# TensorE's column-half blocks in one run per pass, with the banks and the copy order that go with it

## The reference

```python
qkv = x @ W_attn + b_attn                       # x: 2 x 2048 x 256, 16 heads of 16
scores = einsum('bhtd,bhsd->bhts', q, k) / 4    # causal, and s >= t - 64
out = softmax(scores) @ v ; x = layernorm(x + out @ W_proj + b_proj)
expert_idx = argmax(softmax(x @ Wr.T))          # 8 experts
inter = gelu(x @ W1[expert_idx] + b1[expert_idx])
y = layernorm(inter @ Wo + bo + x) * gamma + beta ; result = layernorm(x + y)
```

## Time and profile before

| | us |
|---|---|
| median of 3 executions | 529.68 (529.24 to 534.57) |
| profiled execution | 528.38 |
| its span, first to last instruction | 526.7 |
| TensorE busy | 489.4 (93%) |
| VectorE busy | 431.5 (82%) |
| ScalarE busy | 356.5 (68%) |
| POOL busy | 315.4 (60%) |
| mean granted TensorE clock | 0.979 |

### The profile page before, as it was taken

The page is one execution under the profiler, slowest core; times in us unless marked ns, Lnnn a source line. Parts: engine busy times, 40 slices in busy tenths (PEclk is TensorE's granted clock), DMA queues, the critical chain, the costliest instruction groups (busy, mean ns, idle before and its releaser), DMA issues. The chain is left out here.

```text
span 526.7 us, 24512 instructions
## 1 busy us (share of the span) xinstructions
PE 489.4 (93%) x8574; PEld 432.2 (82%) x8574; DVE 431.5 (82%) x1132; ACT 356.5 (68%) x796; POOL 315.4 (60%) x553
## 2 busy tenths in 40 slices
PE   6989999999999999899978898999999999999980
PEld 5878888788888888688866787888999989999970
DVE  6558798878987898669898567999999989999983
ACT  5677778777876878467867664566667757666860
POOL 8612446444464545434634347777888878888883
PEclk9999999999999999989999898999999999999996
DMA  8687688786977797768772122222235554442200
GB/s 200 165 245 198 185 220 205 204 217 180 259 211 213 196 255 197 188 191 222 174 205 72 44 61 62 71 64 63 77 105 183 206 182 162 163 147 71 53 25 7
DMA packets 90184, 80.96 MB, mean 154 GB/s; under 512 B 36502, under 2 KB 83871, under 8 KB 90018
## 3 DMA queue, kind: packets, MB, share of 16 engines
q1 hardware_dynamic: 86720, 70.95, 48.9%
q0 software_dynamic: 3248, 8.41, 4.7%
q10 hardware_dynamic: 98, 0.04, 0.0%
HBM read 43.50 MB, written 23.55 MB: 127 GB/s over the span
## 5 line engine op out<-in xcount | busy, mean ns | idle before, releaser
L1415 PE MATMUL ps<-v_even,w_hi 128*128 128x128 f16 x1024 | 142.1, 220 | 0.6 <-issue 0.3
L1397 PE MATMUL ps<-wo_hi,ks 128*128 128x256 f16 (+1 forms) x576 | 129.2, 274 | 6.4 <-DVE ks L1091 6.1
L834 ACT ACTIVATE probs<-ps,b1T 128x128 f32<-128x128 f32 (+1 forms) x312 | 85.8, 361 | 66.9 <-PE ps L1415 66.7
L1415 PE MATMUL ps<-v_even,w_lo 128*128 128x128 f16 x512 | 108.6, 220 | 0.1
L1415 PEld LDWEIGHTS ps<-v_even,w_hi 128*128 x1024 | 97.2, 98 | 3.4 <-issue 1.3
L1162 DVE TENSOR_REDUCE mx<-ps 128x4 bf16<-128x512 f32 x128 | 82.5, 682 | 3.7 <-PE ps L1466 2.5
L1397 PE MATMUL ps<-wo_lo,ks 128*128 128x256 f16 (+1 forms) x288 | 78.9, 274 | 0.0
L1091 DVE TENSOR_TENSOR ks<-probs,ks 128x512 f16<-128x512 f32 (+1 forms) x72 | 70.9, 985 | 5.9 <-ACT ks L841 5.6
L853 ACT ACTIVATE probs<-ps 128x512 f32<-128x512 f32 x128 | 69.5, 610 | 5.3 <-PE ps L1492 4.4
L1515 PE MATMUL ps<-v_odd,probs 128*64 128x17 f32 x1024 | 69.4, 210 | 2.0 <-issue 2.0
L744 POOL CAST att_hi<-att 128x256 f16<-128x256 f32 x27 | 10.7, 395 | 100.9 <-DVE att L1219 100.9
(11 more groups left out here) (248 smaller groups left out, 1283.3 us busy)
## 6 DMA issues: line engine op xcount, KB each, us to landing
qk_s<-qk_room SPq DMA_DIRECT2D x32, 256.0 KB, 2.7
w_in<-in_L_ffn_W_dram SPq DMA_DIRECT2D x16, 512.0 KB, 5.7
v_odd<-slots SPq DMA_DIRECT2D x64, 128.0 KB
qs<-qk_s SPq DMA_DIRECT2D x16, 384.0 KB
ks<-qk_s SPq DMA_DIRECT2D x16, 384.0 KB, 5.5
ks<-qk_s SPq DMA_DIRECT2D x32, 144.0 KB, 3.2
v_even<-v_odd SPq DMA_DIRECT2D x63, 68.0 KB, 3.1
qk_s<-qk_room SPq DMA_DIRECT2D x32, 128.0 KB, 2.7
```

The costliest lines, as they stand in the source:

```text
L834: last = nc.scalar.activation(g[1 - p][:, ic, n * w:(n + 1) * w], ps_h[1 - p][:, half, col + n * w:col + (n + 1) * w], ACT.Gelu, bias=b1T[ ...
L1397: ins = mm(ps_y[p][0:m], h[p][hs][:, ic, 0:m], wo[ws][:, ic, :], start=n == 0, stop=n == 3 * IC - 1)
L1415: up_ins = mm(ps_h[1 - p][:, half, col + m * w:col + (m + 1) * w], weights(ws, m, k, ic), sT[1 - p][ss][:, k, at], start=k + n == 0, stop= ...
```

## The change

On TensorE the projection and the turn of x now stand in front of scores 0 and 1, so that scores 0 and 1, values 0, scores 2 and 3 and values 1 follow each other (only pass 0 keeps the scores first). The maxima's tile is 128 wide instead of 32, so its transposes are too, and ScalarE reads the first 32 partitions of the result. The projection writes bank 6 (the values' bank) except for the last tile, the ranks bank 2 except for the last pair, x's turn bank 4. On VectorE y and logits stand before maxima 0, `router_x` behind attT and waits for the product instead of the copy; the low halves of w1 come as two in even passes (one right behind mean and variance, one behind `router_x`) and none in odd ones. On ScalarE the last exponential of a tile and the copy of v stand in the next pass, behind x's high part, and exponential 0 stands behind the high part of queries and keys.

```diff
-        mx = [sb(f"mx{k}", [P, P - ALIGNED], bf16) for k in range(2)]
+        mx = [sb(f"mx{k}", [P, P], bf16) for k in range(2)]
...
-            return ps[:, 0 if t >= LEAD else 4 + t % 2, 0:CC * P].rearrange("p (k t) -> p k t", k=CC)
+            return ps[:, 4 if t >= LEAD else 4 + t % 2, 0:CC * P].rearrange("p (k t) -> p k t", k=CC)
...
-        ps_proj = ps[:, 1, 0:C + E]
+        def ps_proj(t):
+            return ps[:, 6 if t < TILES - 1 else 1, 0:C + E]
...
-        ps_rank = ps[:, 1, 320:320 + 3 * E].rearrange("p (a e) -> p a e", a=3)
+        def ps_rank(pair):
+            return ps[:, 2 if pair < TILES // 2 - 1 else 1, 320:320 + 3 * E].rearrange("p (a e) -> p a e", a=3)
...
+        def w1_lows(it):
+            lows_at = range(it - 2, it if it % 2 == 0 else it - 2) if it < TILES - 3 else w1_halves(it)
+            return [n for n in lows_at if a_tile(n)]
... ScalarE
                 for t in turned(it) if it > FIRST else ():
                     x_high(t)
+                if a_tile(it - 1) and it < LAST - 2:
+                    exps(3, it - 1)
+                if a_tile(it) and it > 0:
+                    copy_v(it)
...
-                if a_tile(it + 1):
-                    m = it + 1
-                    act.wait_ge(v_done, m + 1)
...
-                if cur:
-                    exps(0)
...
                 if cur:
+                    exps(0)
                     exps(1)
-                if cur:
                     exps(2)
-                    exps(3)
... VectorE
-                    dve.wait_ge(v_out, m + 1)
+                    dve.wait_ge(v_done, m + 1)
...
+                for n in w1_lows(it)[:1]:
+                    split_w1(n)
...
-                for n in w1_halves(it):
+                if it >= 0 and a_tile(it + 1):
+                    router_x(it + 1)
+                for n in w1_lows(it)[1:]:
                     split_w1(n)
... TensorE
-                        wait(pe, att_done, done)
+                        wait(pe, lg_done, done)
...
-                    wait(pe, lg_done, old + 1)
                     wait(pe, v_out, m)
-                    wait(pe, lx_done, m)
...
                 if it == 0:
                     warm(10)
-                scores(0)
+                    scores(0)
+                    scores(1)
                 if a_tile(old):
                     pe.wait_ge(attT_out, old + 1)
...
-                scores(1)
                 for t in turned(it):
                     pe.wait_ge(xin_ld[t % 3], 16 * (t // 3 + 1))
                     if t >= LEAD:
-                        pe.wait_ge(qkh_done, t)
-                        pe.wait_ge(qkl_done, t)
+                        wait(pe, exp_done, 4 * (it - 1) + 1)
...
+                if it != 0:
+                    scores(0)
+                    scores(1)
                 values(0)
                 scores(2)
                 scores(3)
...
-                    pe.wait_ge(v_out, upto(it + 1))
-                    pe.wait_ge(lx_done, upto(it + 1))
+                    if a_tile(it):
+                        pe.wait_ge(mxT_out, 2 * it + 2)
```

More of the change, by code:

```diff
@@ L859, in maxima_rows, with copy_v @@
                     nc.scalar.activation(q.rearrange("p (i h) n -> p i h n", i=STRIPS),
-                                         ps_mx.rearrange("p e m n -> p (e m) n").unsqueeze(1)
+                                         ps_mx[0:P - ALIGNED].rearrange("p e m n -> p (e m) n").unsqueeze(1)
                                          .broadcast_to([P - ALIGNED, STRIPS, 2 * CC, BLK]),
                                          ACT.Copy, scale=1.0 / ONE).then_inc(mxT_out, 1)
+                def copy_v(m):
+                    act.wait_ge(v_done, m + 1)
+                    act.wait_ge(lx_done, m + 1)
+                    if m == 0:
+                        act.wait_ge(v_clear, 1)
+                    wait(act, pv_done, CC * (m - VRING + 1))
+                    wait(act, vtop_ld[m % 2], 16 * ((m - VRING) // 2 + 1))
+                    wait(act, vlow_ld[(m + 1) % 2], 16 * ((m - VRING) // 2 + 1))
+                    nc.scalar.activation(
+                        v_odd[m % VRING][:, :, 0:HD], ps_v[:, 0:C].rearrange("p (h d) -> p h d", d=HD), ACT.Copy)\
+                        .then_inc(v_out, 1)
                 new, sent = it + LEAD, it - 3
                 if it == LAST - 2:
+                    exps(3, it - 1)
                     nc.scalar.activation(table_in[:, :], zero[0:1, :], ACT.Gelu)
@@ L946, in _ @@
                         copy_rows(1, e, t)
+                    copy_v(0)
             walk_slots(body3)
@@ L1180, in router_x @@
                 def router_x(m):
-                    dve.wait_ge(v_out, m + 1)
+                    dve.wait_ge(v_done, m + 1)
                     wait(dve, lg_done, m - 3)
                     nc.vector.tensor_tensor(lx[:, m % 4, :], ps_v[:, C:C + E], lb[:, :], ALU.add).then_inc(lx_done, 1)
+                if a_tile(old):
+                    dve.wait_ge(proj_done, old + 1)
+                    dve.wait_ge(xrb_done, old + 1)
+                    wait(dve, x1_done, old - 1)
+                    nc.vector.scalar_tensor_tensor(y[old % 2][:, :], ps_proj(old)[:, 0:C], W_DOWN, xin[old % XRING],
+                                                   ALU.mult, ALU.add).then_inc(y_done, 1)
+                    dve.wait_ge(lx_done, old + 1)
+                    wait(dve, is_top_done, old // 2)
+                    nc.vector.tensor_tensor(logits[:, old % 2, :], ps_proj(old)[:, C:C + E], lx[:, old % 4, :], ALU.add)\
+                        .then_inc(lg_done, 1)
                 maxima(0)
@@ L1189, in _ @@
                     x_low(t)
[L1190 to L1199, removed]
                 if it == FIRST:
@@ L1440, in scores @@
                     if step == 0:
+                        wait(pe, place_done, (done - 1) // 2)
                         pe.wait_ge(stack_ld[pair % 2], 16 * (pair // 2 + 1 + window_loads(pair)))
@@ L1538, in _ @@
                     warm(10)
-                scores(0)
+                    scores(0)
+                    scores(1)
                 if a_tile(old):
                     pe.wait_ge(attT_out, old + 1)
-                    wait(pe, v_out, upto(it))
-                    wait(pe, lx_done, upto(it))
-                    wait(pe, place_done, old // 2)
+                    if old == TILES - 1:
+                        pe.wait_ge(v_out, TILES)
+                        pe.wait_ge(place_done, old // 2)
                     if old == 0:
                         pe.wait_ge(wlo_done, 4)
-                    product(ps_proj, [(attT[:, 0, c, :], attT[:, 1, c, :]) for c in range(CC)],
+                    product(ps_proj(old), [(attT[:, 0, c, :], attT[:, 1, c, :]) for c in range(CC)],
                             [(wp[0][:, c, :], wp[1][:, c, :]) for c in range(CC)]).then_inc(proj_done, 1)
-                scores(1)
                 for t in turned(it):
@@ L1659, in _ @@
                     pe.wait_ge(onehot_done, old // 2 + 1)
[L1660 to L1663 removed]
+                    if a_tile(it):
+                        pe.wait_ge(mxT_out, 2 * it + 2)
+                    if old == TILES - 1:
+                        pe.wait_ge(lg_done, TILES)
+                    rank = ps_rank(old // 2)
+                    both = rank[:, 0:2, :].rearrange("p a e -> p (a e)")
                     mm(both, before[:, :], onehot[:, 1:3, :].rearrange("p a e -> p (a e)"), start=True, stop=False)
                     mm(both, ones_b[:, :], onehot[:, 0:2, :].rearrange("p a e -> p (a e)"), start=False, stop=True)
[L1666 to L1667 removed]
+                    mm(rank[:, 2, :], ones_b[:, :], onehot[:, 1, :], start=True, stop=False)
+                    mm(rank[:, 2, :], ones_b[:, :], onehot[:, 2, :], start=False, stop=True).then_inc(rank_done, 1)
                 scores_t(2)
```

22 lines of the change are left out of this document (5 added, 17 removed).

## The result

| | before | changed |
|---|---|---|
| median, us | 530.44 (529.24 to 534.57, 4 runs) | 549.15 (546.76 to 555.41, 4 runs) |
| ratio, 95% interval | | 1.0324 [1.0243, 1.0405] |
| profiled execution, span | 528.38, 526.7 | 546.76, 545.0 |
| granted TensorE clock, mean | 0.979 | 0.958 |

The changed kernel is 3% slower; the forecast was 522.5, within 514 to 532. The ratio compares executions in the same state and leaves out the changed kernel's longest, 555.41.

A forecast was written before the change was run, and what follows sets the result against it. TensorE's issue order was taken to set the 8.15 us pass. Saving 0.46 us a pair over 13 pairs (6.0) plus 1.2 in the tail, 7.2, gave 521.2 profiled, 522.5 as median; range 514 to 532.

The forecast's parts named there:

- TensorE's own saving: Attention loop: six column-width changes fewer per pass take 0.65 us off TensorE's work, 8.15 to 7.50 us.
- the sum: All terms added: a pair of passes from 16.30 to 15.84 us over 13 pairs, plus 1.2 in the tail, 7.2 together.
- About 26 passes (tiles 2 to 27) in that state: Attention loop: these passes were taken to last 8.15 us each, with TensorE busy throughout.
- Maxima's wider load, nothing: Maxima's transposes: the weight load four times wider runs under the matmuls and costs nothing.
- Logits before values 0, 0.07 us a pass: Projection in the values' bank: y and logits must empty it before values 0, losing 0.07 us per pass.
- The four tail passes are VectorE's; they get y and logits earlier: Passes from 257 to 297 us: VectorE bounds them, and the change gains 1.2 us there.
- Head and FFN: 0: Outside the attention loop: the change costs or gains nothing in the head and the FFN.
- att_lo blocked, 0.3 us a pair: Even passes: a w1 split starting first delays POOL's att_lo, so the transposes of attention start later; 0.3 us taken.
- Window loads, 0.3 us a pair: Odd to even handover: window loads behind v's late copy land late for scores 1 and 2; 0.3 us taken.
- the slower rival: Odd pass: copy, v transfers, L469 landing late, scores 1 waiting; 7 us more, 537 us; chance 0.13.
- the walk down SyncE's queue: Odd pass: v's transfers, then L469 and L486 behind the late copy, followed to their landings; 0.3 us a pair taken.

The follow-up runs named there:

- number 9: number 8 with the projections of all passes from 28 on in bank 1: 535.09 us, ratio 1.0050.
- 10: number 9 with W1's low parts made one in each pass, as before the change: 531.75 us, ratio 0.9972.
- 14: Changed kernel with v copied early and the last passes' projections in bank 1; low parts two in even passes, W1 loads whole: 528.22 us, ratio 0.9994.
- 13: 10 with W1 loaded whole, 512 KB in odd passes, instead of in halves: 526.18 us, ratio 0.9962.
- Number 7: Kernel before, with SyncE holding v's transfers and all behind them until ScalarE has read the pass's x: 539.7 us, ratio 1.0127.
- number 1: Changed kernel with v copied early, in the pass that made it, as before the change: 531.73 us, ratio 1.0086.
- number 8: Changed kernel with v copied early, tile 30's projection in bank 1 and W1 loaded in halves, one in each pass: 535.12 us, ratio 1.0057.

## Why the prediction was wrong, step by step

- **TensorE's own saving: right.** The projection's 264-column block, the maxima's transposes and scores 0 and 1 with their switch hold 0.68, 0.11 and 0.53 to 0.57 us in undisturbed passes. By the sum's terms an odd pass was to be 7.57 (7.50 and the logits' 0.07) and an even one 7.87 (with att_lo's 0.3 too); the undisturbed ones take 7.56 and 7.88. A change of column width costs what was read from the earlier trace rows, 0.10 to 0.12 us each way. The Trainium skill (TensorEngine Tiling (Array Packing), Key Properties) says that a change of the tiling mode drains TensorE; the trace agrees in that each change costs time, and does not show what the time is spent on.
- **The pass that was read was not the usual one.** "About 26 passes (tiles 2 to 27) in that state" took two passes for all. The 24 periods of the kernel before took 205.2 us and not 24 times 8.15, 195.6: TensorE lost nearly 10 us there already, 3.7 of it in stops for instructions and 3.4 at half clock. The waits of that trace would have shown the three stops, and with them a limit that no term of the sum and no rival has.
- **Maxima's wider load, nothing: right.** The transposes hold 0.11 us.
- **Logits before values 0, 0.07 us a pass: right in the loop, if anything less** (waits of 0.9 us in all), **wrong in the tail.** "The four tail passes are VectorE's; they get y and logits earlier": VectorE's list has the slot tables ahead of them there. This is a term that I left out, 5.5 us of waits and a part of the half clock around them, where the sum had a gain of 1.2 us. The windows of the earlier trace rows said that VectorE was the longer one there; the new wait should have been set against that list in particular. "Head and FFN: 0" fails by the same wait in the pass of tile 30 and by the clock around it, at 0.50 up to 318.4 us, where the FFN has begun; how the 2.2 us behind the last projection divide was not followed.
- **att_lo blocked, 0.3 us a pair: right as a wait.** The weight loads wait 3.1 us over 11 even passes, mean 927 ns and not 680. That taking it away saves time is not shown: the ratio falls by 0.008 from number 9 to 10 and by 0.003 from 14 to 13, with intervals that overlap, and neither loop is shorter in the traces.
- **Window loads, 0.3 us a pair: less.** TensorE waited 2.1 us for ks<-qk_s over the loop, in three waits, nearly all of it for the second block's keys. The two loads landed in 3.5 and 4.9 us at the median, where 3.9 and 5.5 had been taken, and the mechanism of the slower rival, scores 1 waiting for L469, is not what happened.
- **The step that failed** is the walk down SyncE's queue: it stopped at the transfers that a matmul waits for. W1, x and the stores behind them were named in the rival ("w1's 512 KB now follow L486 directly and the stores of q and k come behind them") and priced only by what they do to L469's landing. They have no reader that is in a hurry, so they were counted free. But they share the 16 DMA engines with TensorE's instructions, and in the kernel before 6 of 38 blocks already came with nothing to spare, with the DMA engines busy 0.97 of an odd pass. Waits for issue went from 3.7 to 14.0 us and half clock cost 3.4 us more; with the shorter waits above, and what each stop costs beside its record, the loop lost 20 us. That overturned the forecast.
- **The other half of it** is the saving itself. Number 7 shows that the late queue alone costs 1.3%; the changed kernel loses 3.2% and more if its saving is counted. Faster passes ask for the instructions sooner while the same transfers run; number 1, with the queue on time, still has 18 of 38 blocks with nothing to spare. That this is why the sum is larger is argued from the table, not shown: no run changed TensorE's rate and nothing else.

What stays open: which property of the bunch (its bytes, its count of small packets, the stores' writes) delays the instruction packets; how much of the 9.3 us that number 1 still waits comes from its denser order; and what the short waits for issue off the raster are.

## What to carry to other kernels

A transfer that nobody waits for is not free in a kernel whose DMA engines are busy: when a wait on the issuing queue moves, follow every transfer behind it until the queue is level again, and look at which of them now run together. "Issue" waits of a microsecond in the middle of a TensorE block, with no semaphore at that place, were late instructions here: see whether their places lie multiples of 256 records apart, and compare them with the instruction queue's packets, before looking for a cause in the kernel's order. Short ones need not be: 12 of the 17 in number 8 were not on the raster. Read more than two passes before calling a period typical. And a wait added to a loop must be checked against its exceptional passes, where an engine's list is not the usual one.

## What the runs showed of the hardware that was not expected

- TensorE can stand still for 1 to 2 us for want of instructions in a straight run of matmuls: ten times and 12.2 us in 212 us of the changed kernel, at places that are multiples of 256 records apart, each stop ending 1.3 to 1.5 us behind a 16 KB packet of queue q8.
- Such a stop can cost twice: at four of the ten a stretch of about 3.4 us at 1.2 GHz began.
- 6.4 MB of loads less, of 81 MB, changed one kernel's time by 2% and the other's by nothing that can be measured.
